# Graph layer, mixer and routed experts on one core: the last two routing batches become one, and the units left as filler start later

## The reference

```
x = x + gnn(xn, src, dst, edge_weight) + mix(xn)          # 212,500 edges
gnn:  neighbor = segment_sum(w * xn[src], dst)
      out = leaky(xn@W1.T + b1 + (neighbor + neighbor*xn)@W2.T + b2); out / norm(out)
mix:  linear attention over all tokens, then gelu(ret@w1+b1)@w2 + b2 + xn
h = _layernorm(x)
ffn:  idx = argmax(h@gate_w + gate_b), one of 8 experts, at most CAP tokens each
      y = prob * (relu(h@w1[idx] + b1[idx]) @ w2[idx] + b2[idx])
x = x + nan_to_num(y)
```

## Time and profile before

| | us |
|---|---|
| median of 3 runs | 2525.07 (2523.99 to 2526.01) |
| the profiled execution | 2525.24 |
| its span | 2523.5 |
| TensorE busy in it | 2059.4 |
| GpSimd busy in it | 1845.6 |
| VectorE busy in it | 1518.1 |
| ScalarE busy in it | 1035.9 |
| mean granted clock of TensorE | 0.923 |

### The profile page before, as it was taken

One profiled execution on the slowest core, in us unless ns is written; L12 is line 12 of the kernel. 1 busy time (PEld: TensorE's weight loads), 2 busy tenths in 40 slices (PEclk: granted clock), 3 DMA queues, 4 the chain that ended last, 5 costly groups with the idle time before them and its releaser, 6 DMA issues. The chain is left out here.

```text
span 2523.5 us, 42709 instructions
## 1 busy us (share of the span) xinstructions
PE 2059.4 (82%) x12889; PEld 1588.6 (63%) x12889; DVE 1518.1 (60%) x5334; ACT 1035.9 (41%) x2482; POOL 1845.6 (73%) x1920
## 2 busy tenths in 40 slices
PE   0049999994677778999989999898889989786797
PEld 0015666662455656777767777677777777676686
DVE  6776555554467776787646656656557657554232
ACT  4663333330244444553433433444444444442232
POOL 7777777777777777777777777777777777743574
PEclk9999999996788888999999989999999999897899
DMA  9846666664566667777677777777888888776652
GB/s 340 314 137 177 175 175 174 175 170 130 158 194 197 200 193 252 233 250 227 224 244 248 228 231 227 250 225 251 305 292 290 314 298 293 258 290 219 250 163 84
DMA packets 279341, 571.22 MB, mean 226 GB/s; under 512 B 51253, under 2 KB 180030, under 8 KB 259679
## 3 DMA queue, kind: packets, MB, share of 16 engines
q0 software_dynamic: 97776, 266.80, 34.9%
q1 hardware_dynamic: 150945, 250.43, 29.1%
q10 hardware_dynamic: 30390, 51.21, 5.5%
HBM read 506.22 MB, written 87.99 MB: 235 GB/s over the span
## 5 line engine op out<-in xcount | busy, mean ns | idle before, releaser
L950 POOL DMA_INDIRECT rows_sb<-xn_scratch,src_sb x1517 | 1459.4, 962 | 462.7 <-issue 457.9
L1244 PE MATMUL bank<-acc 128*128 128x128 f32 (+1 forms) x2624 | 444.4, 323 | 5.5 <-ACT acc L2007 4.0
L1268 PE MATMUL bank<-acc 128*128 128x256 f32 x1680 | 414.9, 391 | 0.0
L1244 PEld LDWEIGHTS bank<-acc 128*128 128x128 f32 x2624 | 388.9, 206 | 30.4 <-issue 6.5
L1062 PE MATMUL bank<-rows_sb,s_sb 128*24 128x256 f32 x3082 | 229.0, 418 | 199.2 <-DMA rows_sb<-xn_scratch,src_sb 193.1
L2024 ACT ACTIVATE acc<-bank,acc 128x128 f32<-128x128 f32 (+1 forms) x656 | 211.9, 398 | 375.5 <-PE bank L1244 375.2
L1268 PEld LDWEIGHTS bank<-acc 128*128 128x128 f32 x1680 | 314.6, 194 | 50.1 <-issue 1.1
L1532 DVE TENSOR_TENSOR acc<-acc,bank 128x48 f32 x831 | 170.4, 205 | 277.1 <-PE bank L1072 161.9
L1062 PEld LDWEIGHTS bank<-rows_sb,s_sb 128*24 128x24 f32 x3082 | 85.5, 107 | 272.8 <-issue 229.1
L1945 ACT COPY sums<-bank 120x256 f32<-120x256 f32 x208 | 76.4, 367 | 354.7 <-PE bank L1062 353.9
L1976 ACT ACT_TABLE_LOAD x95 | 121.9, 1283 | 193.4 <-PE bank L1151 192.6
(11 more groups left out here) (272 smaller groups left out, 3638.2 us busy)
## 6 DMA issues: line engine op xcount, KB each, us to landing
acc<-ffn_first_in SPq DMA_DIRECT2D x66, 1028.0 KB
acc<-ffn_w_in SPq DMA_DIRECT2D x66, 1024.0 KB
arena<-xn_scratch SPq DMA_DIRECT2D x194, 128.0 KB, 3.1
h_scratch<-arena ACTq DMA_DIRECT2D x97, 256.0 KB
rows_sb<-xn_scratch,src_sb POOLq DMA_INDIRECT x1517
xnt_scratch<-arena SPq DMA_DIRECT2D x97, 128.0 KB, 2.3
arena<-xnt_scratch SPq DMA_DIRECT2D x97, 128.0 KB
arena<-x_in SPq DMA_DIRECT2D x97, 128.0 KB
```

Of the source, the lines that this page charges most:

```text
L950: pool.indirect_dma_start(out=chunk_row(c), out_offset=None, in_=xn_d, in_offset=bass.IndirectOffsetOnAxis(ap=src_sb[:, c:c + 1], axis=0)) ...
L1244: m = pe.matmul(bank[:, i * tokens:(i + 1) * tokens], w1_sb[k % 2][:, h, f * P:(f + 1) * P], xt[:, k % 2, h, 0:tokens], start=h == 0, stop ...
L1268: m = pe.matmul(bank[:, i * D:(i + 1) * D], hid[:, f, i * P:(i + 1) * P], w2_sb[k % 2][:, f, :], start=False, stop=f == FC - 1 and i == 0)
```

## The change

It has five parts:

1. The batches' ends are cut from the end in a first step of 7 instead of 3. The two last batches become one, tiles 91 to 97, with 22 units (60 to 81), chosen at place 215, slots at 218. There are 18 batches; `SINGLE_BATCHES` goes from 9 to 8, so the same units are of one tile. `MOST_SLOTS` makes room for 22 columns.
2. `SKIPS` leaves out the first four units of the last batch instead of two: GpSimd loads the weights from unit 64 on.
3. `most_ticks` allows no tick in places 208 to 211, one in each place from 212 on, and two at place 216. In places from 216 on a place's first tick goes ahead of its other steps. The planner then gives: unit 56 in places 212 and 213, unit 57 in 214 and 215, (58,1) and (58,2) in 216, (59,1) in 217, (59,2) in 218, nothing in 219, and unit 60 from place 220 on. The last place is 265.
4. The returns are scattered four a place in places 209 to 218 (40 tiles), and the other 37 two a unit from unit 62 to unit 80.
5. The first three back loads stand at place 208 instead of 209, and SyncE does a place's back loads ahead of its unit loads. Back loads 3 to 7 then stand at places 211, 213, 215, 217 and 219, loads 8 and 9 at 231 and 239.

```diff
--- before.py
+++ after.py
@@ -54,7 +54,7 @@
     LAP_W = LAP + WIN
     UNIT = UNIT_TILES * P
     SLOTS = (N + NE * (P - 1)) // P
-    SINGLE_BATCHES = 9
+    SINGLE_BATCHES = 8
     FLUSH = 2
     RT = 4
     RB = 7
@@ -290,7 +290,7 @@
         e_wide = behind(0, P)
         hot_e = behind(0, NE)
         counted = behind(0, NE)
-        MOST_SLOTS = 20
+        MOST_SLOTS = 22
         sel = behind(1, 2 * MOST_SLOTS)
         load_row = behind(1, MOST_SLOTS).bitcast(I32)
         sprb = behind(0, SLOTS)
@@ -447,7 +447,7 @@
 
 
         dense = [t for t in range(RB, T, RB) if enters[t] == FIRST_C + t]
-        ends = dense + list(range(T - 3, dense[-1] + RT - 1, -RT))[::-1] + [T]
+        ends = dense + list(range(T - RB, dense[-1] + RT - 1, -RT))[::-1] + [T]
         routes = [range(a, b) for a, b in zip([0] + ends, ends) if a < b]
         assert T > 3 and all(len(v) <= RB for v in routes)
         chosen_at = [enters[v[-1]] + C_STEPS - 1 for v in routes]
@@ -512,7 +512,7 @@
 
         LAST = len(routes) - 1
         FINAL = [k for k in range(K) if batch_of[k] == LAST]
-        SKIPS = FINAL[2:]
+        SKIPS = FINAL[4:]
         assert len(FINAL) % 2 == 0 and LAST in queued
 
         def small_steps(p, at_end):
@@ -554,7 +554,7 @@
         sums_at = [p + 1 for p in chosen_at]
 
         def most_ticks(p):
-            return 2 if p < PAIRS or p in sums_at or p - 1 in sums_at else 1
+            return 2 if p < PAIRS or p in sums_at else p >= PAIRS + 4
 
         e_place, time, p = [], 0.0, FIRST_C
         wanted_at = [slots_at[b] + (4 if slots_at[b] + 4 < PAIRS else 2) for b in batch_of]
@@ -582,7 +582,7 @@
         for n, (k, j) in enumerate(e_ticks):
             here = at_place(e_place[n])
             after = next((i for i, v in enumerate(here) if v == ("late", e_place[n])), len(here))
-            if e_place[n] in sums_at and e_place[n] >= PAIRS and ("unit", n - 1) not in here:
+            if e_place[n] >= max(PAIRS, sums_at[-1]) and ("unit", n - 1) not in here:
                 here.insert(0, ("unit", n))
             elif ("unit", n - 1) in here or after == len(here):
                 here.append(("unit", n))
@@ -628,8 +628,8 @@
         scatter_at = [[k for k in v if k >= len(kept)] for v in scatter_at]
         backs = [range(a, min(a + BACK_ROWS, kept_tiles)) for a in range(0, kept_tiles, BACK_ROWS)]
         keepers = [[k for k in kept if set(columns_of(k)) & set(v)] for v in backs]
-        quiet = [p for p in range(PAIRS + 1, last_c + 4) for _ in range(4)]
-        tail = [place_of(k, 1) for k in range(K) if place_of(k, 1) > last_c + 4]
+        quiet = [p for p in range(PAIRS + 1, last_c + 1) for _ in range(4)]
+        tail = [place_of(k, 1) for k in range(K) if place_of(k, 1) > last_c + 4][:-1]
         each = -(-(kept_tiles - len(quiet)) // len(tail))
         quiet += [p for p in tail for _ in range(each)]
         back_at = [[] for _ in range(PLACES)]
@@ -639,7 +639,7 @@
         back_place = {col: p for p in range(PLACES) for col in back_at[p]}
         back_ld_at = [[] for _ in range(PLACES)]
         for i in range(len(backs)):
-            back_ld_at[PAIRS + 1 if i < BACK_SLOTS else back_place[backs[i - BACK_SLOTS][-1]] + 1].append(i)
+            back_ld_at[PAIRS if i < BACK_SLOTS else back_place[backs[i - BACK_SLOTS][-1]] + 1].append(i)
 
 
         def y_value(k):
@@ -852,6 +852,8 @@
                                 load_rows(t)
                             elif t + LAP_TILES < T:
                                 load_acc(t + LAP_TILES)
+                for i in back_ld_at[p]:
+                    load_back(i)
                 for k in w1_at[p]:
                     if k not in SKIPS:
                         load_first(k)
@@ -860,8 +862,6 @@
                         load_second(k)
                 for k in keep_at[p]:
                     keep_unit(k)
-                for i in back_ld_at[p]:
-                    load_back(i)
             for t in range(max(0, T - OS), T):
                 sp.wait_ge(c_st[t % OS], 32 * (t // OS + 1))
```

## The result

The changed kernel takes 2506.17 us, median of 5 runs (2502.10 to 2510.89), against 2525.07 (2522.51 to 2526.01): ratio 0.9926, 95% interval 0.9911 to 0.9941. The forecast was 2504.6. The profiled execution took 2506.76 with a span of 2505.0 us.

A forecast was written before the change was run, and what follows sets the result against it. The end was taken as a sum: unit 60's start, 22 units, their stalls, an unchanged tail. Unit 60 at 2311.3, plus 162.8, 1.7 and 3.0, gives 2478.8; with 24.05 and 1.74, 2504.6 us; range 2495 to 2522.

The forecast's parts named there:

- Places without units: Places 208 to 211: two loops of 4.95 us; last tile ends at 2249.1 instead of 2254.10, giving 5.0 us.
- rival A: Places 209 to 218: idle gaps keep TensorE at its lower clock; 2513.7 us, chance 0.17.
- the 2.5 taken between 0 and 7.8: Places 208 to 211: allowance in us for three products at a possibly low clock, 2.6 more each at worst.
- From there to unit 60: Last tile's end to unit 60's first product: 60.7 us of path plus 1.5 for late weights; unit 60 at 2311.3.
- The load time: 1 MB weight loads: median 7.3 us taken from the profile over the skill's 4.4, which would make the sum 1.5 lower.
- The run: Unit 60 to unit 81: 162.8 us at dense pace, 1.7 lower clock, 3.0 stalls; unit 81 at 2478.8.
- B: Units 57 to 63: back loads ahead of unit loads make weights late; five stalls give 2532.6 us, slower; chance 0.11.
- C: Places 212 to 218: each takes 3 us more through ScalarE and VectorE; 2525 us, no change; chance 0.06.
- D: Better case: no late weights, no stalls, full clock from place 208; 2497.6 us, chance 0.13.
- the next back load stands 12 places on: Run of 22 units: a reason given why the weight gaps of 4.83 and 6.57 us should go.
- theory 1: Expectation for experiments: the gain is the merging, filler's place worth a few us; merging alone gives 2508 to 2515 us.
- the filler that filled places 208 to 211 is now on this path, 11.5 longer: Last tile to unit 60: 60.7 us against 49.2 before, as moved filler covers a wait only in part.

The follow-up runs named there:

- m4: Changed kernel with SKIPS = FINAL[2:], so GpSimd loads the weights from unit 62 on instead of 64: ratio 0.9929.
- m1: Kernel before with only parts 1 and 2 (merged last batch and its four SyncE weights), filler and returns as before: 2519.1 us, ratio 0.9982.
- m3: Changed kernel with parts 4 and 5 undone: first back loads at place 209 behind unit loads, scatters up to place 221: 2514.59 us, ratio 0.9958.
- m6: Changed kernel with only the lines `quiet` and `tail` undone, four scatters a place up to place 221 again: ratio 0.9952.
- k1: m1 plus only `quiet` and `tail` as changed, so scatters of four a place end at place 218: ratio 0.9947.
- m2: Changed kernel with the filler ticks of units 56 to 59 back in places 208 to 215, one a place: 2504.2 us, ratio 0.9919.
- n1: Changed kernel with the eight filler ticks split: five in places 208 to 212, three in the holes of the routing chain: ratio 0.9898.

## Why the prediction was right

The mechanism and the size held; the account of which edit does it did not. That the time came out so close is partly luck: from the last pair's transposes to the end the terms sum to 273.2 us, and so do the measured distances, but the four terms (to the last tile, to unit 60, the run, the tail) miss by -0.3, -1.1, +1.8 and -0.3 us.

*Places without units.* Predicted 19.4 us from the last pair's transposes to the end of the last tile's products, measured 19.1 (2231.79 to 2250.88). The two loops took 5.15 and 6.6 (ends at 2239.12, 2244.27 and 2250.88). Cut at about these ends, with the 7.9 us behind them as the last row, the changed kernel's stretches read (columns as above):

```profile
2231.80:2239.00 7.20, 6.65 (x26) 5.65 (x26) 2.67 (x11) 0.37 (x1) 3.28 (x4) 0.61 0.98 368
2239.00:2244.30 5.30, 3.33 (x19) 2.81 (x17) 2.96 (x10) 4.01 (x8) 4.08 (x5) 1.00 0.54 183
2244.30:2250.90 6.60, 4.50 (x16) 2.97 (x15) 3.34 (x11) 1.27 (x5) 5.08 (x6) 0.76 0.65 206
2250.90:2258.80 7.90, 2.61 (x14) 2.31 (x15) 6.08 (x21) 1.55 (x6) 6.07 (x7) 0.72 0.97 382
```

The second loop's products of lines 1149 and 1151 take 1.69 and 1.91 us for four matmuls:

```profile
2242.34 1.03 PE L1149 MATMUL bank<-w1g_sb,arena 128*128 128x256 f32 x4
2243.20 1.03 PE L1151 MATMUL bank<-w2g_sb,arena 128*128 128x256 f32 x4
...
2247.45 1.69 PE L1149 MATMUL bank<-w1g_sb,arena 128*84 128x256 f32 x4
2248.93 1.91 PE L1151 MATMUL bank<-w2g_sb,arena 128*84 128x256 f32 x4
```

Against 1.03 and 1.03 in the loop before it, that is 1.5 us. So of rival A it is right that the clock falls again in this half-idle stage, and the clock was back at full level in between: A was right in kind, but the 9 us by which it stood over the forecast did not come, and the 2.5 taken between 0 and 7.8 was a little high. The fall came inside the burst of the second loop and not ahead of it: granted 1.00 from 2246.50 to 2247.60, 0.51 from there to 2250.90.

The rule of the Trainium skill, "TensorE: Matmul & The Clock Gate", section "HAM oscillation — how this bites in real kernels", is that a burst behind a wait starts slow. Neither loop bears it out, as both started at a granted 1.00 right behind 1.97 and 2.10 us of idle. The first tick does: behind 2.77 us of idle, sixteen matmuls took 3.76 us.

```profile
2257.31 3.76 PE L1244 MATMUL bank<-acc 128*128 128x128 f32 x16 [2.77 <-ACT acc L2007]
```

*From there to unit 60.* Predicted 62.2, measured 61.1. The steps: sums done 30.0 and 29.7; first table product 42.0 and 42.8; indices written 52.4 and 53.3; from the index to the product 8.3 and 7.9. The weights of unit 58 were late as taken (1.5): second weights issued at 2276.33, the bias product waited 2.03 us until 2284.63. The row names line 2024 as releaser, but ScalarE had ended that at 2283.77, 0.86 earlier, so I put it down to the load; the trace does not name it. In m4 the same product waited 3.53 us, and there the row names no engine.

```profile
2282.63 1.14 ACT L2024 ACTIVATE acc<-bank,acc 128x128 f32<-128x128 f32 x4 [0.32 <-PE bank L1244]
```

*The load time.* Taken so, that load took 8.3 us from issue to product, near the 7.3 of the earlier trace rows, and the median decided rightly. By the formula of the Trainium skill, "DMA: Bandwidth & Descriptors", section "Anatomy of one DMA — SWDGE (gpsimd) path", an estimated 4.4 us, it would have landed at 2280.7 and nothing would have waited. The page gives that formula for one DMA issued by GpSimd; this load is SyncE's, and three more transfers of 1 MB were issued within 5 us of it.

*The run.* Predicted 167.5 for 21 units with clock and stalls, measured 169.3. Stalls were 1.04 and 1.73, and about 1.7 of lower clock behind the second: 4.5 against the 3 taken.

*The rivals.* B, C and D did not occur; no place took 3 us more than added up. B's mechanism is real, though. m1, m3, m6 and k1 each lost 2 to 6 us a time to weights behind a back load. It was named for units 57 to 63 as a danger of the new order. For units 60 to 63 the new `quiet` is what removes it, and the old one kept it.

*What failed* is one step: that "the next back load stands 12 places on", so that the gaps of 4.83 and 6.57 should go, stands in the prediction without the edit that gives it, and theory 1 put it down to the merging. m1 has the merged batch and a gap of 5.24 instead. The next back load stands 12 places on only because `quiet` ends at `last_c`, an edit that has no term of its own in my sum; for the returns I had only the 1.5 us for the weights of unit 58. And "the filler that filled places 208 to 211 is now on this path, 11.5 longer" charged the path for ticks that m2 shows to cost the same on the other side: with ticks in 208 to 215 unit 60 comes after 80.4.

## What to carry to other kernels

Where one queue issues, in order, both transfers that the next work needs and transfers that wait for another engine's progress, look first at what stands behind each wait: moving one back load from ahead of the weights gave 0.35% here (k1 against m1), where the whole merging of two routing rounds gave 0.18%. Filler paid here where it stood inside a wait of the critical chain, a tick for a hole: put all before or all around the chain, it gave the same time, and split over the holes it gave 0.3%. Undo an edit that moves the end of a range by three places separately: its cost hides in what else is computed from that range.

## What was not expected of the hardware

The last pair's transposes, up to which the order of work is the same in all kernels, started at 2229.66 to 2236.39 us in the fourteen profiled executions, a spread of 6.7 us that is a third of the whole gain, while the distance from the last tick to the span's end was 20.2 us in each of the twelve with the merged batch.

A 1 MB load that SyncE issued 1.1 to 1.4 us after a back load, and that TensorE then waited for, took 8.0 to 11.9 us from issue to product (m6 8.0, changed 8.3, m1 8.6 and 10.1, m4 8.9, m3 9.1, n1 9.5, before 10.0 and 11.9, m2 10.6, k1 10.9), where the median of the earlier trace rows is 7.3. Only loads that came late can be timed so, which makes them look slower than all of them are.
